# Where VectorE turns the second and fourth pair of gathered token blocks in a mixture-of-experts kernel

## What is computed

```
x_rotated = hamilton(q_left_n, hamilton(x_filtered, q_right_conj))
scores = softmax(x_rotated @ gate_w.T);  topv, topi = top_k(scores, 2);  gates = topv / sum(topv)
loc = running count of the tokens of each expert;  valid = loc < cap          # cap = 1024
disp[topi * cap + loc] += x_rotated                                           # 8 experts x 1024 slots x 512
h = relu(einsum('ecd,ehd->ech', disp, fc1_w) + fc1_b)                         # 2048 hidden
eo = einsum('ech,ehd->ecd', h, fc2_w) + fc2_b
out = x + sum over the two experts of gates * eo
```

## Time and profile before

| | us |
|---|---|
| three timed runs: median (lowest to highest) | 1586.12 (1583.0 to 1586.63) |
| the profiled execution | 1586.64 |
| its span, first to last instruction | 1584.9 |
| PE busy (share of the span) | 1416.6 (89%) |
| DVE busy | 1074.1 (68%) |
| ACT busy | 709.3 (45%) |
| POOL busy | 383.0 (24%) |
| mean granted TensorE clock | 0.939 |

### The profile page before, as it was taken

The page is one execution under the profiler, slowest core; times in us unless marked ns, Lnnn a source line. Parts: engine busy times, 40 slices in busy tenths (PEclk is TensorE's granted clock), DMA queues, the critical chain, the costliest instruction groups (busy, mean ns, idle before and its releaser), DMA issues.

```text
span 1584.9 us, 17933 instructions
## 1 busy us (share of the span) xinstructions
PE 1416.6 (89%) x6095; PEld 1148.1 (72%) x6095; DVE 1074.1 (68%) x1632; ACT 709.3 (45%) x1072; POOL 383.0 (24%) x322
## 2 busy tenths in 40 slices
PE   8548989979898899979899798989899798999997
PEld 5326867868776778758778587767788587788885
DVE  6786758656685768747686567847587476866543
ACT  5234445434463435444454344634454444544442
POOL 1061112520052210531025200522105310240011
PEclk9667999989999899989999899999999899999999
DMA  8465464564555554564635645555545635354232
GB/s 314 155 146 120 81 137 98 168 141 93 115 135 159 118 125 90 153 162 85 141 106 168 132 94 116 142 151 117 125 93 153 156 81 103 103 167 81 52 94 92
DMA packets 452141, 200.45 MB, mean 126 GB/s; under 512 B 398816, under 2 KB 401001, under 8 KB 450130
## 3 DMA queue, kind: packets, MB, share of 16 engines
q1 hardware_dynamic: 429922, 132.27, 37.4%
q0 software_dynamic: 22128, 67.03, 13.6%
HBM read 159.50 MB, written 39.98 MB: 126 GB/s over the span
## 4 chain that ended last, share of the span: by engine, by line
PE 62%; DVE 14%; DMA 11%; SPq 4%; issue 4%; POOL 3%; ACT 1%; DVEq 0%; POOLq 0%; ACTq 0%
PE ps L1025 11%; PE ps L1026 11%; PE ps L1030 11%; PE ps L1002 9%; PE ps L1004 8%; PE ps L1003 8%; DMA x_blk<-in_x,gather_row 4%; SPq L228 4%; DMA slots_dram<-x_blk 3%; DMA x_blk<-slots_dram 2%; DVE w_lo L745 2%; POOL rows L368 1%; DVE yfull L801 1%; DVE yfull L789 1%; DVE h L816 1%
## 5 line engine op out<-in xcount | busy, mean ns | idle before, releaser
L1002 PE MATMUL ps<-yc_hi,w1c_hi 128*128 128x512 f32 x896 | 360.9, 403 | 103.1 <-DVE h L877 100.7
L1025 PE MATMUL ps<-w_hi,h_hi 128*128 128x512 f32 x960 | 383.3, 399 | 4.1 <-issue 2.4
L1026 PE MATMUL ps<-w_lo,h_hi 128*128 128x512 f32 x960 | 380.2, 396 | 0.0
L1003 PE MATMUL ps<-yc_lo,w1c_hi 128*128 128x512 f32 x896 | 357.7, 399 | 0.0
L1004 PE MATMUL ps<-yc_hi,w1c_lo 128*128 128x512 f32 x896 | 357.7, 399 | 0.0
L1002 PEld LDWEIGHTS ps<-yc_hi,w1c_hi 128*128 128x128 f32 x896 | 173.2, 193 | 147.7 <-DVE h L877 106.6
L1030 PE MATMUL ps<-w_hi,h_lo 128*128 128x512 f32 x960 | 256.8, 389 | 0.0
L1025 PEld LDWEIGHTS ps<-w_hi,h_hi 128*128 128x128 f32 x960 | 186.1, 194 | 49.6 <-issue 5.3
L1026 PEld LDWEIGHTS ps<-w_lo,h_hi 128*128 128x128 f32 x960 | 185.2, 193 | 39.2
L1030 PEld LDWEIGHTS ps<-w_hi,h_lo 128*128 128x128 f32 x960 | 180.5, 188 | 37.9
L1004 PEld LDWEIGHTS ps<-yc_hi,w1c_lo 128*128 128x128 f32 x896 | 173.6, 194 | 37.2
(11 more groups left out here) (160 smaller groups left out, 1578.2 us busy)
## 6 DMA issues: line engine op xcount, KB each, us to landing
w_raw<-in_L_ffn_fc_w SPq DMA_DIRECT2D x256, 256.0 KB
w_raw<-in_L_ffn_fc_w SPq DMA_DIRECT2D x512, 64.0 KB
slots_dram<-x_blk POOLq DMA_DIRECT2D x28, 512.0 KB
x_blk<-slots_dram SPq DMA_DIRECT2D x224, 64.0 KB
out<-x_all SPq DMA_DIRECT2D x8, 1024.0 KB, 12.6
x_all<-in_x SPq DMA_DIRECT2D x7, 1024.0 KB, 13.3
b_bc<-in_L_ffn_fc_b POOLq DMA_DIRECT2D x8, 256.0 KB
x_all<-in_x SPq DMA_DIRECT2D x4, 256.0 KB, 3.9
```

The lines of the kernel that those rows point to most:

```text
L1002: pe.matmul(bank, hi, yc_hi[:, y, q, :], start=first and q == 0, stop=False, skip_group_check=True)
L1003: pe.matmul(bank, hi, yc_lo[:, y, q, :], start=False, stop=False, skip_group_check=True)
L1025: pe.matmul(eo_s[:, b, :], h_hi[:, c, blk], w2_hi[:, w, :], start=False, stop=False, skip_group_check=True)
L1026: pe.matmul(eo_s[:, b, :], h_hi[:, c, blk], w2_lo[:, w, :], start=False, stop=False, skip_group_check=True)
```

## The change

Two of the four `turn_x` calls of each expert move on DVE from the middle of their group to its end: `turn_x(4e + 1)` in group 1 and `turn_x(4e + 3)` in group 5 now stand behind `w1_low(G + 2)`. `turn_x(4e)` and `turn_x(4e + 2)` stay, and so does every instruction of PE, ACT, POOL and SP. Seven of the eight experts have these calls (the last has no next expert), so 14 calls of two transposes move.

```diff
                     w2_low(N)
                     if not last:
-                        if g < 2:
-                            turn_x(4 * e + g)
-                        elif g < 5:
+                        if g == 0:
+                            turn_x(4 * e)
+                        elif 1 < g < 5:
                             rotate(e + 1, 0, g - 1)
-                        elif g == 5:
-                            turn_x(4 * e + 3)
-                        else:
+                        elif g > 5:
                             rotate(e + 1, 1, g - 5)
...
                     if G + 2 < E * GROUPS:
                         w1_low(G + 2)
+                    if not last and g == 1:
+                        turn_x(4 * e + 1)
+                    if not last and g == 5:
+                        turn_x(4 * e + 3)
                 for tile in range(HT):
```

## The result

| | before | changed |
|---|---|---|
| timed runs, us: median (lowest to highest) | 1586.38 (1583.0 to 1591.39) | 1495.12 (1492.76 to 1500.6) |
| the profiled execution | 1586.64 | 1492.76 |
| its span | 1584.9 | 1491.0 |
| mean granted TensorE clock | 0.939 | 0.966 |

The ratio is 0.9427, with a 95% interval of 0.9391 to 0.9464. The forecast was 1494 us, 92.7 less in the profiled execution; it became 93.9 less.

The account below looks back on a forecast made before the run. PE was taken as the bound except at 14 stops costing 134.9 us. Eight stops giving 55.1 us and six giving 37.6 make 92.7 us, and 1586.64 - 92.7 = 1494 us, range 1477 to 1521.

Parts of the forecast that it names:

- What bounds the kernel: PE is the bound except where 14 stops in groups 1 and 5 halt it, costing 134.9 us.
- Group 5, and group 1 of e = 0: Eight stops: DVE's wait goes, a stop of 0.5 us remains at S3, no slow clock booked; 55.1 us go.
- Group 1 of e = 1 to 6: Six stops: pieces land late, DVE still waits 3.0 us, a 3.46 us stop remains at S3; 37.6 us go.
- 6.26 holds six times: Group 1 of e = 1 to 6: of 12.16 us too many, 6.26 go in each, 37.6 us together.
- The clock: Slow clock behind each of the six remaining 3.46 us stops: bounds 0 and 2.44 us, 2.44 taken.
- the clock holds: Rival: a 3.46 us stop does not bring the lower clock, 14.6 us more go, 1479 us; chance 0.15.
- SP: SP's order stays, so weights may come late; 0 booked, bound 2 us for each of 13 places (26 us).
- The signs: PE's wait for line 875 falls to a few us, s2 wait some 22, DVE's about 18; groups 15.5 and some 21.
- signs of being wrong: DVE waits anew for weights before line 723, PE waits for w_lo, or group 1 still takes over 23 us.
- no effect: Rival: the landing of the pieces times the program, PE's wait only moves from line 877 to s2; 1586 us, chance 0.03.
- slower: Rival: the turn delays gather, store and SP's cut, so stops return one group later and longer; 1600 or so, chance 0.04.
- The weights come late: Rival: SP's cut stands in front of weights that are wanted sooner; 1520 us with the 26 us bound, chance 0.18.

Follow-up runs that it names:

- all three edits: Changed kernel with first_of_slab late on ScalarE, two cuts behind the weights on SyncE, pair 4e + 1 gathered before result rows on GpSimd; 1451.42 us, ratio 0.9144.
- run with set stops: Changed kernel with 7 to 12 extra ScalarE copies ahead of s2 in groups 1 to 6 of the last expert; one execution, 1509.8 us.
- kernel with SyncE's cuts late: Changed kernel with the loads of pieces first in SyncE's groups 2 and 6 moved to the end of these groups, behind the weights; ratio 0.9371.
- GpSimd's order changed: Changed kernel with GpSimd gathering pair 4e + 1 ahead of the next slab's result rows instead of behind them; ratio 0.9267.
- ScalarE's: Changed kernel with ScalarE's first_of_slab moved from the end of groups 1 and 5 into groups 2 and 6, behind w2_high(N); ratio 0.9273.
- middle place: Changed kernel with the two moved turns behind line 875 and w2_low(N + 1), ahead of turn_w1 and the weight sums; ratio 0.9716.

## Why the prediction was right

**What bounds the kernel**: right. The 134.9 us of the 14 stops were the thing to win, and with all of them gone (all three edits) the span fell by 135.9 us.

**Group 5, and group 1 of e = 0**: right to 0.1 us a group. The stop that stays was put at 0.5 us, and the groups lose 0.40; 55.9 us went where the sum has 55.1.

**Group 1 of e = 1 to 6**: right in its mechanism (DVE's remaining wait, the chain over `first_of_slab` and `s2`, the stop at S3). The length was 4.43 us for 4.56. The six idle times were 3.17 in e = 1 where 3.46 was worked out, and 2.79 to 5.65 in the others. The term "6.26 holds six times", 37.6 us, measured 75.8 - 35.9 = 39.9: within it the clock's price of 2.44 was too high. By the same count (group less 14.96 less idle time) it is 1.7 to 1.9 in five stops and 3.0 in one. The term holds as a sum and not six times: from e = 1 to 6 the groups gave 7.1, 6.1, 7.9, 3.8, 7.2 and 7.9 us, since the pieces landed 16.2 to 19.1 us after the start of group 1 where it had been 16.3 to 17.7.

**The clock**: the choice of 2.44 over 0 was right. The rival "the clock holds" fell, since all six stops paid, also the one of 2.79 us. But it was nearer than its chance of 0.15 may suggest. Stops of up to 2.49 us cost nothing in the last expert of the run with set stops, and in the kernel with SyncE's cuts late the same stop of e = 2, there 3.32 us, cost nothing beyond itself (last section). That all six paid was in part luck. Of the 2.44 us a stop, 0.30 is no clock either, but idle time that the record hides.

**SP**: "I book 0, with a bound of 26 us" measured 2.7 us. The place was foreseen, the weight turn of group 7 in front of the second phase; DVE's wait for weights is 2.8 us in 5 places. The step that failed is "on PE the second phase follows, without need of these weights": a late turn there reaches PE by `w_lo`, a few tenths in most experts, 1.4 us in e = 4, where DVE waits 1.32 us for a half of the weights. SP's issue times came as worked out: the second cut of e = 1 at 345.43 before would be at 330.1 on the clock of the changed kernel (its group begins 15.34 us sooner, at 301.67), and it was issued at 329.74, with the weights behind it:

```profile
329.74 5.33 SPq L228 DMA_DIRECT2D x_blk<-slots_dram  x8
335.11 1.10 SPq L263 DMA_DIRECT2D w_raw<-in_L_ffn_fc_w  x2
336.25 5.35 SPq L228 DMA_DIRECT2D w_raw<-in_L_ffn_fc_w  x8
```

**The signs** named for the new profile came, with two slips of naming: ACT's `s2` keeps its line number (526, not 524), and the stops stand in the windows of groups 2 and 6, not 1 and 5. DVE's wait was to be 18 us or more and is 22.3; the new wait of PE was to be some 22 us and is 23.6; the disturbed groups were to take 15.5 and some 21 us and take 15.36 and 19.66 to 23.64. The signs of being wrong came too, all three, in small: DVE waits anew for weights before line 723 (2.8 us), PE's wait for `w_lo` grew from 1.7 to 5.9 us, and the group behind the turn took over 23 us in e = 4 (23.64). The first two had no size with them; measured, they are the 2.7 us of the second phases and one late landing.

**The other rivals**: "no effect" and "slower" are out by the result. "The weights come late" came true in small: it was worth 2.7 us here, 5.9 with GpSimd's order changed and 11 with ScalarE's.

**The closeness is part luck.** The forecast has 92.7 us and the span fell by 93.9, but two terms were too low, by 0.8 and 2.3 us, and the weights, booked at 0, took 2.7 back.

## What to carry to other kernels

A wait need not be shortened to be worth less: it can be moved in its engine's queue to where the least is queued behind it, and its price is then worked out again from there. Here 96 of 135 us went though the transfers landed no sooner after their group's start than before, on average (17.3 us in group 1 of e = 1 to 6, before 16.8). Follow each thing behind the new place, on the other engines too: in the middle place the same transposes let PE's product go and still gave half of it back, over the weight sums and ScalarE. When a stop goes, look for the queue that had slack only because of it, since SyncE's order cost 3 us in the changed kernel and 6 or 11 once the next stop had been shortened on GpSimd or ScalarE.

## What the runs showed of the hardware that was not expected

The lower clock need not set in at the stop. In e = 1 of the changed kernel PE stops until 322.68, starts again at the upper level, and falls to the lower one (1.2 GHz) some 1.4 us later, for 3 us. The windows around it, granted clock in the column behind the brackets:

```profile
320.60:324.10 3.50, 1.42 (x6) 1.20 (x7) 0.88 (x2) 3.03 (x6) 1.15 (x2) 0.99 0.93 174
324.30:327.20 2.90, 2.90 (x8) 2.30 (x7) 2.90 (x6) 1.12 (x2) 0.70 (x1) 0.50 0.42 86
327.60:332.00 4.40, 4.40 (x21) 3.65 (x20) 4.25 (x9) 2.45 (x4) 3.49 (x4) 1.00 0.44 137
```

So a first matmul of 0.50 us behind a stop (0.79 in the earlier trace rows) does not tell that the upper clock was kept.

Nor does the length alone decide it, between about 1.8 and 3.3 us. Stops of 1.93 and 2.54 us in the kernel with the turn in a middle place lost 1.6 us more to the clock, stops of 2.43 and 2.60 in the kernel with the pair ahead of the rows lost none. The longest one that lost none is the 3.32 us of e = 2 in the kernel with SyncE's cuts late, longer than the 3.17 above. Its first matmul, and the window of its group:

```profile
493.57 0.50 PE L1004 MATMUL ps<-yc_hi,w1c_hi 128*128 128x512 f32 x1 [3.32 <-issue]
```

```profile
487.37:505.97 18.60, 15.28 (x68) 12.31 (x66) 12.58 (x19) 9.40 (x14) 8.76 (x8) 1.00 0.73 167
```

The group took 3.64 us more than 14.96, the stop plus 0.32. In the windows of all these kernels the clock stayed at the upper level in every group whose stops were shorter than 1.8 us, and fell in every one with a stop longer than 3.4 us. What decides in between no run here shows. The Trainium skill says on its page "TensorE: Matmul & The Clock Gate", section "What's actually happening", that the point at which the clock switches varies from run to run for the same kernel. That agrees with stops of like length that cost and did not.
